# Router sums from float32r halves of the turned rows, their copies moved, and an inverse root in PSUM

## What is computed

```python
# attention over the 256 channels of an image, 8 heads, a window of 16 positions
q = Wq @ layernorm(x) + bq;  k = Wk @ ctx + bk;  v = Wv @ ctx + bv
x = x + tanh(g_xattn) * (Wo @ window_attention(q, k, v) + bo)
# router: each channel row (2048 long) is a token, 64 experts, the 8 best
flat   = layernorm(x)                        # (16*256, 2048)
logits = flat @ router_weight.T + router_bias
w      = top8(softmax(logits))
x      = x + tanh(g_ffn) * (flat * sum(w) + w @ expert_bias)
```

## Time and profile before

| | |
|---|---|
| profiled execution, device time | 1549.06 us |
| its span | 1547.0 us |
| median of the three runs | 1548.85 us |
| mean granted TensorE clock | 0.974 |
| TensorE busy | 1457.9 us (94%) |
| VectorE busy | 1232.8 us (80%) |
| GpSimd busy | 1160.6 us (75%) |
| ScalarE busy | 1156.2 us (75%) |
| waits of ScalarE for keys to copy out (L590) | 57.1 us in 50 waits |

### The profile page before, as it was taken

How to read it: one execution, slowest core, us unless ns; L and a number is a source line. 1 busy time by engine, 2 the same in 40 slices (tenths; PEclk the granted TensorE clock), 3 DMA queues, 4 the chain that set the end, 5 groups by cost and what they waited for, 6 DMA issues and landing times.

```text
span 1547.0 us, 66674 instructions
## 1 busy us (share of the span) xinstructions
PE 1457.9 (94%) x28162; PEld 1196.4 (77%) x28162; DVE 1232.8 (80%) x2938; ACT 1156.2 (75%) x2025; POOL 1160.6 (75%) x1126
## 2 busy tenths in 40 slices
PE   4799999999999999999999999999999999999986
PEld 3577877878887888888788888878888887778764
DVE  5477887878888787888888788888878888787774
ACT  3588877778787877888787787878778787767652
POOL 4587777788777878778787887878788787677661
PEclk9799999999999999999999999999999999999896
DMA  7454455554545555454555545455554545434232
GB/s 231 122 127 107 127 149 140 145 161 113 162 131 140 144 154 162 112 161 133 140 144 154 162 114 162 131 140 147 152 161 114 160 133 140 123 82 134 57 77 90
DMA packets 365576, 210.39 MB, mean 136 GB/s; under 512 B 294496, under 2 KB 295520, under 8 KB 361056
## 3 DMA queue, kind: packets, MB, share of 16 engines
q1 hardware_dynamic: 365280, 206.14, 49.1%
HBM read 136.88 MB, written 33.55 MB: 110 GB/s over the span
## 4 chain that ended last, share of the span: by engine, by line
PE 60%; DVE 19%; issue 6%; ACT 6%; POOL 5%; DMA 2%; SPq 1%; POOLq 0%; ACTq 0%; DVEq 0%
PE ps_j L1123 26%; PE ps_s L1183 9%; PE ps_a L1148 7%; PE ps_r L1225 6%; PE ps_s L1123 5%; DVE prob_t L908 4%; DVE st_x L915 2%; PE ps_s L1178 2%; POOL prob L495 2%; PE ps_a L1202 2%; PE ps_t L1165 1%; PE ps_a L1203 1%; DMA x_in<-x_dram 1%; DVE st_in L820 1%; DVE nt_x L814 1%
## 5 line engine op out<-in xcount | busy, mean ns | idle before, releaser
L488 POOL TENSOR_TENSOR score<-score,p_inv 128x384 f32<-128x384 f32 x256 | 219.2, 856 | 110.5 <-DVE p_inv L902 107.6
L495 POOL TENSOR_TENSOR prob<-score,prob 128x384 f16<-128x384 f32 x256 | 262.6, 1026 | 32.8 <-ACT prob L660 31.6
L1183 PEld LDWEIGHTS ps_s<-kv_win,q_col 32*32 32x32 f32 x16384 | 197.2, 106 | 59.2 <-issue 58.7
L1183 PE MATMUL ps_s<-kv_win,q_col 32*32 32x48 f32 x16384 | 233.8, 205 | 4.0 <-issue 3.8
L908 DVE STREAM_TRANSPOSE prob_t<-prob 128x512 f32<-128x512 f32 x256 | 177.1, 701 | 68.0 <-POOL prob L495 67.4
L469 POOL TENSOR_TENSOR c_lo<-c_in,c_hi 128x1024 fp32r<-128x1024 f32 x64 | 152.7, 2385 | 91.0 <-ACT c_hi L634 91.0
L1148 PEld LDWEIGHTS ps_a<-prob_t,v_diag 128*128 128x128 f16 x6528 | 175.8, 98 | 51.0 <-DVE prob_t L908 34.0
L1148 PE MATMUL ps_a<-prob_t,v_diag 128*128 128x48 f16 (+2 forms) x6528 | 188.3, 183 | 26.9 <-DVE prob_t L908 20.2
L464 POOL TENSOR_TENSOR att_lo<-att,att_hi 128x512 fp32r<-128x512 f32 x128 | 161.7, 1275 | 50.1 <-ACT att_hi L620 48.8
L598 ACT ACTIVATE kv_win<-ps_j,v_bias 128x512 f16<-128x512 f32 x128 | 108.2, 847 | 104.0 <-PE ps_j L1123 104.0
L1123 PE MATMUL ps_j<-c_hi,wkv_hi 128*128 128x512 f32 x512 | 172.5, 419 | 14.1 <-POOL c_lo L469 7.0
(11 more groups left out here) (149 smaller groups left out, 3320.0 us busy)
## 6 DMA issues: line engine op xcount, KB each, us to landing
v_diag<-v_turn SPq DMA_DIRECT2D x512, 68.0 KB
c_in<-ctx_dram SPq DMA_DIRECT2D x64, 512.0 KB, 4.9
x_in<-x_dram SPq DMA_DIRECT2D x64, 512.0 KB, 5.7
x_res<-x_dram SPq DMA_DIRECT2D x64, 512.0 KB, 4.7
out_dram<-x SPq DMA_DIRECT2D x32, 1024.0 KB, 8.0
c_sq<-ctx_dram SPq DMA_DIRECT2D x60, 512.0 KB, 5.6
x<-ctx_dram SPq DMA_DIRECT2D x4, 512.0 KB, 7.0
x<-experts_dram SPq DMA_DIRECT2D x2, 512.0 KB, 10.2
```

Source lines behind the costliest of these rows:

```text
L488: pool.tensor_tensor(score[:, u], score[:, u], p_inv[:, u, :].unsqueeze(2).to_broadcast([P, HALF, KEYS]), ALU.mult).then_inc(pm_rdy, 1)
L495: pool.tensor_tensor(part(prob[:, u % 2], 1)[:, :, 0:KEYS], score[:, u], part(prob[:, u % 2], 0)[:, :, 0:KEYS], ALU.subtract).then_inc(pl_ ...
L1183: ins = pe.matmul(s[head(h), n * KEYS:(n + 1) * KEYS], q_col[head(h), g, at:at + SUB], kv_win[c % 2][head(h), 0, g, at:at + KEYS], start=F ...
```

## The change

- `router()` is turned around. The router weights are split once into float32r halves, `wr_both` (64 columns high, 64 low), and become the stationary operand. The turned rows, as `turn_hi` and `turn_lo`, move: 256 columns (two halves of 128 tokens) per matmul, 8 matmuls in a chunk. The sum is 128 rows (64 high, 64 low) x 256 tokens in `ps_r`. `wr_both` is made in the first image by a ScalarE copy (c = 0) and a GpSimd subtraction (c = 1).
- `turn_lo` is new work for VectorE: `turned_low(g)` subtracts `turn_hi` from `ps_t`, 128x512, twice in a chunk. The router, and what next writes `ps_t`, waits for it.
- Once per image (c = 1) ScalarE copies the sums to SBUF (`logit_sums`, 128x256), and `fold_logits` turns them back and adds the two halves with 4 float32 matmuls by the identity, ahead of `router_logits`.
- `copy_rows(0)` goes from the start of ScalarE's step to the step before, behind `high(2)` and ahead of `keys_high(0)`.
- On VectorE `largest(0)` and `shift(0)` go ahead of `stats_in(0)` and `values_turn`; `turned_low(1)` lies between `stats_in(1)` and `largest(0)`, `turned_low(0)` between `stats_x1(0)` and `stats_x1(1)`.
- The router rows' inverse root keeps its variance, half and product in a free part of `ps_r`; the two products of a Newton step are one instruction for each channel half. The router in c = 1 waits for its end.
- `c_sq` has no buffer of its own any more: it lies in `v_turn`. Its load waits until the `v_diag` DMAs have landed, and `values_turn` waits for the square.

```diff
+        c_sq = v_turn[:, :, 0:CHUNK]
-        x1_t = sb("x1_t", [P, G, TB, P])
-        wr = sb("wr", [P, T // P, E])
+        turn_hi = sb("turn_hi", [P, G, TB, P], F32R)
+        turn_lo = sb("turn_lo", [P, G, TB, P], F32R)
+        wr_staged = x1[1][:, 1, 0:(T // P) * E].rearrange("p (n e) -> p n e", e=E)
+        wr_both = sb("wr_both", [P, T // P, 2 * E], F32R)
+        SPARE = 2 * P
+        var_x1, half_x1, nt_x1 = [ps_r[:, SPARE + i * G:SPARE + (i + 1) * G] for i in range(3)]
...
                 if live(b, c, 8):
                     need(sp, sq_rdy, nth(b, c, 7))
-                    sp.dma_start(c_sq[:], rows_in).then_inc(sq_ld, 16)
+                    if live(b, c, 0):
+                        for g in range(G):
+                            need(sp, vd_ld[g], nth(b, c, 0) * (16 * HPG))
+                    sp.dma_start(c_sq, rows_in).then_inc(sq_ld, 16)
...
+                if b == 0 and c == 1:
+                    pool.wait_ge(wrh_rdy, 1)
+                    pool.tensor_tensor(wr_both[:, :, E:2 * E], wr_staged, wr_both[:, :, 0:E], ALU.subtract).then_inc(wrl_rdy, 1)
...
+                def logit_sums():
+                    need(act, r_mm, nth(b, c, -2))
+                    need(act, wd_rdy, 2 * (b - 1))
+                    act.activation(acc, ps_r[:, 0:G * P].rearrange("p (g c) -> p g c", g=G), ACT.Copy).then_inc(acc_rdy, 1)
...
-                if live(b, c, -2):
-                    copy_rows(0, -2)
...
+                if c == 1 and seq(b - 1):
+                    logit_sums()
                 if now:
                     exponent(0)
+                if b == 0 and c == 0:
+                    act.wait_ge(r_ld, 16 * 4)
+                    act.activation(wr_both[:, :, 0:E], wr_staged, ACT.Copy).then_inc(wrh_rdy, 1)
...
                     high(2)
+                if before:
+                    copy_rows(0, -1)
                 if live(b, c, 2):
                     keys_high(0, 2)
...
+            def inverse_root_psum(b):
+                base = (b - 1) * ROOT2
+                dve.tensor_scalar(var_x1, mv_x1[:, :, 1], EPS, None, ALU.add).then_inc(root2, 1)
+                dve.tensor_scalar(half_x1, mv_x1[:, :, 1], EPS, -0.5, ALU.add, ALU.mult).then_inc(root2, 1)
+                dve.tensor_scalar(neg_mean_x1[:], mv_x1[:, :, 0], -1.0, None, ALU.mult).then_inc(root2, 1)
+                dve.wait_ge(root2, base + 2)
+                dve.tensor_scalar(rs_x1[:].bitcast(I32), var_x1.bitcast(I32), -0.5, float(RSQRT_SEED),
+                                  ALU.mult, ALU.add).then_inc(root2, 1)
+                for i in range(3):
+                    dve.wait_ge(root2, base + 4 + 3 * i)
+                    for g in range(G):
+                        dve.scalar_tensor_tensor(nt_x1[:, g:g + 1], half_x1[:, g:g + 1], rs_x1[:, g:g + 1],
+                                                 rs_x1[:, g:g + 1], ALU.mult, ALU.mult).then_inc(root2, 1)
+                    dve.wait_ge(root2, base + 6 + 3 * i)
+                    dve.scalar_tensor_tensor(rs_x1[:], nt_x1, 1.5, rs_x1[:], ALU.add, ALU.mult).then_inc(root2, 1)
+                dve.wait_ge(root2, base + ROOT2)
+                dve.memset(pad[:, 3:4], 0.0).then_inc(ln2_rdy, 1)
...
+                def turned_low(g, off):
+                    need(dve, xt_rdy[g], nth(b, c, off))
+                    need(dve, r_mm, nth(b, c, off - 1))
+                    dve.tensor_tensor(turn_lo[:, g], ps_t[:].rearrange("p (k t) -> p k t", k=TB), turn_hi[:, g],
+                                      ALU.subtract).then_inc(xtl_rdy[g], 1)
...
                 def values_turn(g):
+                    need(dve, sq_rdy, min(nth(b, c, 7), N))
...
                     stats_in(1, ch)
+                if live(b, c, -2):
+                    turned_low(1, -2)
+                if now:
+                    largest(0)
+                    shift(0)
+                if stats:
                     stats_in(0, ch)
                 if now:
-                    largest(0)
                     values_turn(0)
                     values_turn(1)
-                    shift(0)
...
                     stats_x1(0)
+                    turned_low(0, -1)
...
                 def router():
+                    if c == 1 and seq(b - 1):
+                        need(pe, ln2_rdy, b)
+                    need(pe, xtl_rdy[1], nth(b, c, -2))
                     for k in range(TB):
-                        for g in range(G):
-                            ins = pe.matmul(ps_r[:, g * E:(g + 1) * E], x1_t[:, g, k], wr[:, ch * TB + k],
-                                            start=(ch == 0 and k == 0 and g == 0),
-                                            stop=(ch == NCH - 1 and k == TB - 1), skip_group_check=True)
+                        for n, v in enumerate((turn_hi, turn_lo)):
+                            ins = pe.matmul(ps_r[:, 0:G * P].rearrange("p (g c) -> p g c", g=G),
+                                            wr_both[:, ch * TB + k], v[:, :, k],
+                                            start=(ch == 0 and k == 0 and n == 0),
+                                            stop=(ch == NCH - 1 and k == TB - 1 and n == 1))
+                def fold_logits():
+                    need(pe, acc_rdy, b)
+                    for g in range(G):
+                        for i in range(2):
+                            ins = pe.matmul(ps_r[:, g * E:(g + 1) * E], acc[:, g], ident[:, i * E:(i + 1) * E],
+                                            start=(g == 0 and i == 0), stop=(g == G - 1 and i == 1), skip_group_check=True)
+                    ins.then_inc(fo_mm, 1)
...
                     scores(1)
                     scores(2)
+                if c == 1 and seq(b - 1):
+                    fold_logits()
```

More of the change, by code:

```diff
@@ L87, in gated_window_attention_and_router @@
         c_lo = sb("c_lo", [P, G, CHUNK], F32R)
-        c_sq = sb("c_sq", [P, G, CHUNK])
         x_res = sb("x_res", [P, G, CHUNK])
@@ L158, in gated_window_attention_and_router @@
         lg = sb("lg", [P, G, 2, E])
+        acc = lg[:].rearrange("p g j e -> p g (j e)")
         top = sb("top", [P, G, 8])
@@ L220, in gated_window_attention_and_router @@
         r_mm = sem("r_mm")
+        acc_rdy = sem("acc_rdy")
+        fo_mm = sem("fo_mm")
+        wrh_rdy = sem("wrh_rdy")
+        wrl_rdy = sem("wrl_rdy")
         wt_mm = sem("wt_mm")
@@ L250, in gated_window_attention_and_router @@
         xt_rdy = pair("xt_rdy")
+        xtl_rdy = pair("xtl_rdy")
         st1_rdy = sem("st1_rdy")
@@ L343, in _ @@
                              x[0, :, cols(ch)].rearrange("(g p) t -> p g t", g=G)).then_inc(x_ld[ch], 16)
-            sp.dma_start(c_sq[:], ctx[1, :, cols(0)].rearrange("(g p) t -> p g t", g=G)).then_inc(sq_ld, 16)
+            sp.dma_start(c_sq, ctx[1, :, cols(0)].rearrange("(g p) t -> p g t", g=G)).then_inc(sq_ld, 16)
             sp.dma_start(rb[:], rbias.partition_broadcast(P)).then_inc(r_ld, 16)
-            sp.dma_start(wr[:], wrT.rearrange("(n p) e -> p n e", p=P)).then_inc(r_ld, 16)
+            sp.dma_start(wr_staged, wrT.rearrange("(n p) e -> p n e", p=P)).then_inc(r_ld, 16)
             for half in range(2):
@@ L367, in step @@
                     sp.wait_ge(sq_rdy, NCH + 1)
-                    sp.dma_start(c_sq[:], ctx[1, :, cols(1)].rearrange("(g p) t -> p g t", g=G)).then_inc(sq_ld, 16)
+                    sp.dma_start(c_sq, ctx[1, :, cols(1)].rearrange("(g p) t -> p g t", g=G)).then_inc(sq_ld, 16)
                 if live(b, c, 8):
@@ L539, in _ @@
             act.activation(wkv_hi[:, 0], wkv_raw[:, 0], ACT.Copy).then_inc(wkh_rdy, 1)
-            act.activation(x1_t[:, 0], wkv_raw[:, 1].rearrange("p g (k t) -> p (g k) t", t=P), ACT.Square,
+            act.activation(turn_hi[:, 0], wkv_raw[:, 1].rearrange("p g (k t) -> p (g k) t", t=P), ACT.Square,
                            accum_out=w_sq[:, 0:1]).then_inc(wsq_rdy, 1)
@@ L567, in next_square @@
                 act.wait_ge(sq_ld, 16 * (ch + 1))
-                act.activation(c_sq[:], c_sq[:], ACT.Square, accum_out=sq[:, 1, ch:ch + 1]).then_inc(sq_rdy, 1)
+                act.activation(c_sq, c_sq, ACT.Square, accum_out=sq[:, 1, ch:ch + 1]).then_inc(sq_rdy, 1)
             def queries_weight_high(b):
@@ L667, in context_square @@
                     at = (c + 3) % NCH
-                    act.activation(c_sq[:], c_sq[:], ACT.Square,
+                    act.activation(c_sq, c_sq, ACT.Square,
                                    accum_out=sq[:, parity(c, 7, par), at:at + 1]).then_inc(sq_rdy, 1)
@@ L817, in inverse_root @@
                                              ).then_inc(chain if i < 2 else ready, 1)
+            ROOT2 = 13
+            def inverse_root_psum(b):
[15 more added lines that the diff above has]
+                dve.memset(pad[:, 3:4], 0.0).then_inc(ln2_rdy, 1)
             def stats_in(g, ch):
@@ L1035, in step @@
                     need(dve, aggr2, b * (G + 1))
```

(9 more changed lines are left out.)

6 lines of the change are left out of this document (2 added, 4 removed).

## The result

The changed kernel takes 1554.86 us (median of 15 runs, 1550.86 to 1559.76), beside 1548.88 for the kernel before in the same series: a ratio of 1.0037, with a 95% interval of 1.0024 to 1.005. It is 6 us slower; 5 us faster was forecast. The profiled execution took 1555.08 us, its span 1552.9, its mean granted clock 0.973.

What follows compares the result with a forecast made beforehand. TensorE sets the length, with VectorE nearly full in c = 1. 1549.06 + 2.6 + 0.2 - 7.3 - 5.8 - 0.4 + 0.4 + 4.9 = 1543.7, so a median of 1543.5 us; range 1522 to 1574.

Steps and rivals of the forecast that it cites:

- Router, 1.05 us: TensorE's router in each chunk: 1.05 us with 8 matmuls of 256 columns against 1.81 before, gain 0.76.
- Rival C: TensorE's router: the 256-column matmuls cost like 512-column ones, +35 us, 1578; chance 0.07.
- c = 0, c = 1: First two steps of an image: -0.6 us; then +0.5 us, with `attend(1)` waiting about 0.83 for VectorE's transposes.
- c = 2: Third step of an image: the low half is absorbed where VectorE waits for GpSimd anyway; gain 0.70 us.
- c = 3: Last step of an image: `turned_low(1)` waits for ScalarE, the output bias ends 1.0 us later, router gain lost: +1.0 us.
- rival D: Chain in c = 3 isn't lengthened or doesn't hold TensorE: 1528 us, or 1511 with all of the gain; chance 0.20.
- The root in PSUM: c = 1 of images 14 and 15: no hold behind GpSimd, both steps fall to 22.1 us, -7.3 and -5.8.
- rival E: PSUM slows the inverse root by 65 ns in each of 8 dependent steps, 0.5 us in c = 1: 1550.5; chance 0.04.
- Rival A: c = 2: VectorE's L1099 held about 2.2 us by GpSimd's `context_low` in every image: 1572, or 1589 with falling clock; chance 0.18.
- Rival B: The idle stretch in c = 3 costs clock: at 1 us an image, 1558 us; chance 0.13.
- The end: Last router starts 3.2 us later and takes 0.65 less; sums' copy adds 0.6, the fold 1.8: +4.9 us.
- The head: Up to c = 1 of image 1: +0.2 us, for image 0 with its two splittings of `wr`.

Runs made afterwards that it cites:

- locked_235: Kernel after with 52 idle TensorE instructions in each c = 3 and 130 ahead of TensorE's first work: 1543.02 us, ratio 0.9958.
- after_store: Kernel after with the 1 MB stores of finished rows one step later, behind the v_diag transfers and ahead of c_in: 1560.71 us, ratio 1.0058.
- before_drift: Kernel before with 15 idle TensorE instructions in each step, so the borders move by 51 an image instead of 9: 1574.77 us, ratio 1.0165.
- locked_9: Kernel after with 52 idle TensorE instructions in each c = 3 and 100 ahead of TensorE's first work: 1568.75 us, ratio 1.0131.
- no_root: Kernel after with the inverse root back in SBUF, TensorE's program the same length: 1625.45 us, ratio 1.0503.
- alias_only: Kernel before with c_sq in v_turn, its load behind the landing of v_diag, and nothing else: 1548.24 us, ratio 0.9985.
- root_only: Kernel before with the inverse root of the router's rows in PSUM and nothing else: 1534.37 us, ratio 0.9921.
- root_store: Kernel before with the inverse root in PSUM and the stores of finished rows one step later: 1527.37 us, ratio 0.9855.
- locked_61: Kernel after with 52 idle TensorE instructions in each c = 3 and 48 ahead of TensorE's first work: 1564.79 us, ratio 1.0108.

## Why the prediction was wrong

The step that failed stands in its first paragraph: thirteen images take 90.5 us each, "so what holds for one holds for all of them". The sum took one image's waits for all and had no term for TensorE's supply. One such wait lay in the very image of the earlier trace rows, and is the 0.90 us for which TensorE is idle in c = 3:

```profile
757.56 0.56 PE L1148 MATMUL ps_a<-prob_t,v_diag 128*128 128x48 f16 x16 [0.90 <-issue]
```

With the quiet steps of both traces: before, 20.91 + 21.61 + 23.34 + 24.04 = 89.9 an image, 1168.7 for thirteen, and 8.0 of irregular loss, which is what the images took beyond that; after, 89.2 an image, 1159.6, and 26.6 of it. The quiet part gained 9.1 us, where +2.6 was forecast; the irregular part took 18.6. So the sum's other errors, of c = 3 above all, hid 11.7 us of what this one cost: by luck the number came nearer than its steps. Of the 18.6 us the supply waits themselves are 11.7. Some 4 more are two steps in which the clock fell (a c = 3 of 25.65 us and a c = 1 of 24.27, both at 0.93); the rest I didn't assign. locked_235 shows the cause from the other side. With the borders elsewhere the thirteen images take 1172.2 us in its profile in place of 1186.2, and the whole, by the ratios, 0.8% or some 12 us less than after. That the borders' places cost time is shown; which transfers and which clock make one border dear and the next free is shown only in part (after_store, before_drift).

The Trainium skill, "Runtime: NRT & Kernel Launch", Instruction fetch mechanics, says that an engine's instructions come in blocks of 16 KB, 256 of them, through a DMA queue of its own; by this the trace agrees (221 packets, 3.62 MB). It also calls the crossing of a block mostly hidden. Here the measurement decides: up to 2.4 us a crossing (locked_9), in a dense stretch under full DMA engines.

The other steps, in order:

- **Router, 1.05 us.** Right: in c = 3 of the quiet image it runs from 850.28 to the next row's start at 851.32, 1.04 us; and c = 0 at its shortest fell by 0.76, 20.91 to 20.15. Rival C is out.
- **c = 0, c = 1.** -0.76 and +0.4 in the quiet image, for -0.6 and +0.5. The +0.4 is that image's: there `attend(1)` waited 0.68 us for the transposes. In six of the thirteen c = 1 took 21.67 to 21.73 us, +0.1, with a wait of 0.34 to 0.37, so this term was too dear as well.
- **c = 2.** -0.36 for -0.70: `attend(1)` waits 0.48 us for the transposes there, too; the low half wasn't absorbed. A mis-sized term.
- **c = 3.** 0.0 for +1.0. The prediction's chain is there: VectorE's `turned_low(1)` waits 0.59 us for ScalarE's copy, as it said, and the router's gain is lost in the wait for the output bias. But the root is never blocked now. Its last instruction starts 10.53 us into the step both times (761.89 - 751.36, 855.25 - 844.72). Before, two instructions of this root lasted 0.54 and 1.18 us behind GpSimd. I had given 0.3 for that, it was 1.4. So rival D was right on this step.
- **Low half.** About 0.67 us each and never over 0.70, as said.
- **The root in PSUM.** Right: 21.70 and 21.50 us for the predicted 22.1 twice. In c = 1 of images 14 and 15 it gained 14.2 us for 13.1. Three instructions of a Newton step take 0.58 us with PSUM and 0.59 without, so rival E is out. The instruction that closes a step reads PSUM and takes 159 ns, where the one in SBUF takes 161. A product for one channel half takes 222 ns in place of 161, but the two of a step overlap and replace two that waited for each other. What I missed is that without it the change would have cost 70 us more (no_root).
- **Rival A.** L1099 is L1158 after, and took 162 to 165 ns in all sixteen images. c = 2 of image 14 kept its 26.37 us because another instruction there, a cast from SBUF to SBUF, was held:

```profile
L1151 DVE CAST wd_cat<-wd x16: 215/219/2386, 187.9 to 1536.5; 128x128 fp32r<-128x128 f32 x16
```

- **Rival B.** It came true in part: in one of the thirteen c = 3 steps, and in that of image 14. Behind a wait of 1.52 us for the output bias the products slow down:

```profile
480.33:505.98 25.65, 24.13 (x435) 19.23 (x435) 20.46 (x51) 18.41 (x32) 18.62 (x19) 0.93 0.55 156
```

```profile
496.49 0.71 PE L1182 MATMUL ps_j<-c_hi,wkv_hi 128*128 128x512 f32 x2 [1.52 <-ACT x L698]
...
498.64 1.05 PE L1182 MATMUL ps_j<-c_hi,wkv_hi 128*128 128x512 f32 x2
```

  From 497.2 to 500.5 the granted clock is 0.50, and the step takes 1.6 us more than the quiet 24.06. c = 3 of image 14, 23.61 us before, takes 25.91 at 0.93 behind a wait of 1.96; this accounts for the 2.0 us by which the stretch behind the thirteen images missed. In the thirteen images the eleven other waits for the output bias, up to 1.73 us, were followed by no fall, so the length of the wait alone doesn't decide. after_store has six such steps.
- **`c_sq`, and `copy_rows(0)`.** The first costs nothing (alias_only). The second was said to cost nothing in c = 0 to 2, which holds only because the root isn't in SBUF any more (no_root).
- **The end.** +5.4 for +4.9, by the steps given: the router starts at 1526.82, after a wait of 3.39 us for the second `turned_low`, and the fold takes 1.97 us.
- **The head.** +2.0 for +0.2. c = 1 of image 0 takes 20.43 us before (granted clock 1.00) and 24.27 after (0.86), but 24.04 (0.86) in root_only, too, whose new root hasn't run yet. So this needn't come of the change.

## What to carry to other kernels

When an engine of a fully unrolled program is full of short instructions, look at the spread of equal steps before trusting their mean, and number the instructions at each wait that no semaphore explains. If they are 256 apart, removing work can cost time: the number of instructions in a period decides where the borders fall, and large transfers issued just ahead of a dense stretch decide what a border costs. Moving the transfers gained 7 us by the medians and 10 by the ratios (root_store beside root_only), but nothing where an engine had no room for the later load (after_store). Padding the period gained some 12 us with the borders in one place (locked_235) and lost 11 and 15 in two others (locked_61, locked_9), so it has to be tried.

A second one: of a change with several parts, time each alone. The smallest part here, thirteen instructions of one or two elements, gained some 13 us by itself; the large one around it gave more than that back.

## What the runs showed of the hardware that I had not expected

- TensorE runs dry at a border of 256 instructions when its dense stretch uses a block up before the next one is there. The longest wait was 2.4 us (locked_9); behind one of 1.98 the granted clock fell to a mean of 0.81 over the step, which lost 6.7 us (before_drift).
- Idle instructions (waits that are met), 52 to 60 an image, cost nothing where TensorE's products of 512 columns run: the shortest steps didn't move by 0.1 us.
- The instruction that GpSimd holds needn't be a product of two tiles: the one held for 2.39 us in c = 2 of image 14 was a cast of one SBUF tile.
